# Moving the node tables and one-hots into place by DMA, and a second product tap for two channel groups

## The reference

```python
y = affine(conv1x1(x, fc1_w, fc1_b), fc1_s, fc1_t)
nodes = windows of y                                  # 64 nodes per window
idx = knn_idx(nodes, 9)                               # the 9 nearest nodes of each node
x_j = nodes[idx]; x_i = nodes[:, :, None, :]
feat = concat([x_i, x_j - x_i])
h = gelu((einsum('bnkc,oc->bnko', feat, ew) + eb) * es + et)
h = max(h, axis=2)                                    # over the 9 neighbours, 192 channels
x = affine(conv1x1(h, fc2_w, fc2_b), fc2_s, fc2_t) + x
```

```python
h = relu(bn(conv1x1(x, w1)))                          # 96 -> 576 channels
h = relu(bn(depthwise 3x3 (h, wd)))                   # 9 taps per channel
x = x + bn(conv1x1(h, w2))                            # 576 -> 96 channels
```

## Time and profile before

| | us |
|---|---|
| median of 3 runs | 4107.27 |
| lowest, highest | 4103.47, 4110.96 |
| the profiled execution, its own time | 4102.94 |
| its span, first to last instruction | 4101.1 |

### The profile page before, as it was taken

How to read it: one execution, slowest core, us unless ns; L and a number is a source line. 1 busy time by engine, 2 the same in 40 slices (tenths; PEclk the granted TensorE clock), 3 DMA queues, 4 the chain that set the end, 5 groups by cost and what they waited for, 6 DMA issues and landing times.

```text
span 4101.1 us, 79112 instructions
## 1 busy us (share of the span) xinstructions
PE 3901.0 (95%) x22752; PEld 2049.0 (50%) x22752; DVE 3821.5 (93%) x5162; ACT 3694.2 (90%) x6805; POOL 931.2 (23%) x1060
## 2 busy tenths in 40 slices
PE   4999999999999999999999999999999999999984
PEld 2445555455554555555555455555555455555542
DVE  2599999999999999999999999999999999999996
ACT  3899999999998999989999899989999899999983
POOL 0122222122222122222122222122222122222113
PEclk9999999999999999999999999999999999999996
DMA  1133342333333333343333333333333333433333
GB/s 50 24 64 76 58 88 51 67 76 66 73 73 66 60 75 73 58 80 57 69 75 66 73 61 75 62 69 76 62 79 57 70 66 67 81 61 59 62 66 65
DMA packets 100114, 272.31 MB, mean 66 GB/s; under 512 B 14946, under 2 KB 23394, under 8 KB 93476
## 3 DMA queue, kind: packets, MB, share of 16 engines
q0 software_dynamic: 65536, 184.58, 26.4%
q1 hardware_dynamic: 34116, 82.27, 7.5%
HBM read 77.68 MB, written 25.69 MB: 25 GB/s over the span
## 4 chain that ended last, share of the span: by engine, by line
PE 68%; DVE 11%; issue 9%; ACT 9%; DMA 1%; SPq 0%; POOL 0%; DVEq 0%; ACTq 0%; POOLq 0%
PE pg L648 18%; PE pmisc L576 9%; PE pg L651 8%; PE pvu L635 8%; DVE acc L1032 7%; PE pmisc L562 7%; PE pmisc L519 3%; PE pmisc L512 2%; PE pvu L621 2%; ACT MV L807 2%; PE pmisc L578 2%; DVE hid L1010 2%; PE pmisc L542 2%; PE pmisc L547 2%; ACT tapped L844 1%
## 5 line engine op out<-in xcount | busy, mean ns | idle before, releaser
L1032 DVE SCALAR_TENSOR_TENSOR acc<-hpad,w,acc 128x1024 f32<-128x1024 f32 (+1 forms) x2304 | 2618.2, 1160 | 33.5 <-issue 16.3
L648 PE MATMUL pg<-MV,VU 128*128 128x512 f32 x2048 | 1149.2, 643 | 40.7 <-ACT VU L815 29.8
L824 ACT ACTIVATE g<-pg 128x512 f32<-128x512 f32 x1536 | 912.5, 594 | 127.9 <-PE pg L651 81.4
L1010 DVE TENSOR_REDUCE hid<-g 128x192 f32<-128x1536 f32 x512 | 892.6, 1743 | 0.0
L429 POOL DMA_DIRECT2D acc<-tapped x256 | 241.3, 943 | 2106.8 <-DVE acc L1032 1818.8
L807 ACT ACTIVATE MV<-pvu,cst 64x512 f32<-64x512 f32 x1024 | 696.0, 680 | 11.8 <-PE pvu L621 5.0
L576 PE MATMUL pmisc<-acc,w 128*96 128x256 f32 x2048 | 497.1, 386 | 49.0 <-ACT acc L854 34.1
L651 PE MATMUL pg<-MV,VU 128*64 128x512 f32 x2048 | 527.5, 592 | 0.0
L562 PE MATMUL pmisc<-x,w 96*128 96x512 f32 (+1 forms) x1024 | 518.3, 608 | 7.0 <-ACT hpad L766 7.0
L635 PE MATMUL pvu<-wVU,y 97*64 97x192 f32 x4096 | 446.7, 339 | 21.8 <-ACT MV L807 21.2
L576 PEld LDWEIGHTS pmisc<-acc,w 128*96 128x96 f32 x2048 | 331.5, 165 | 262.6 <-issue 154.9
(11 more groups left out here) (101 smaller groups left out, 4447.6 us busy)
## 6 DMA issues: line engine op xcount, KB each, us to landing
acc<-tapped POOLq DMA_DIRECT2D x256, 512.0 KB, 4.9
xin<-in_x_dram SPq DMA_DIRECT2D x32, 768.0 KB, 5.8
invb<-rows_dram SPq DMA_DIRECT2D x32, 768.0 KB
x<-in_x_dram POOLq DMA_DIRECT2D x128, 192.0 KB, 4.4
res<-x POOLq DMA_DIRECT2D x128, 192.0 KB, 5.0
out_dram<-res SPq DMA_DIRECT2D x128, 192.0 KB, 3.2
hpad<-hpad SPq DMA_DIRECT2D x112, 33.0 KB, 1.8
g<-in_consts_dram SPq DMA_DIRECT2D x1, 640.0 KB
```

Of the source, the lines that this page charges most:

```text
L648: last = nc.tensor.matmul(ps[:, :], VU[:, r, part, 0:ONE128], cols[part], start=True, stop=True)
L824: nc.scalar.activation(g[:, p % 2, part, :, :], pg[(3 * p + part) % 2][:, :].rearrange("p (n k) -> p n k", k=KN), ACT.Gelu).then_inc(gelu_ ...
L1010: nc.vector.tensor_reduce(hid[:, c % 2, j, :, :], g[:, r], op=ALU.max, axis=AX.X).then_inc(hid_ready, 1)
L1032: nc.vector.scalar_tensor_tensor(out=dst, in0=src, scalar=wk, in1=dst, op0=ALU.mult, op1=ALU.add).then_inc(tap_done, 1)
```

## The change

**Part 1, the pair's path.** Both blocks of 64 partitions are computed where they fall, and SP's DMAs carry them to where `gather` wants them:

- `values` is one matmul of 384 columns into 128 partitions, one pair earlier (of P+2 in the slot of P); `vu_copy` copies it into the new tile `nodesVU`; four DMAs of 64 partitions by 192 values (`move_tables`) bring it into `VU`.
- `onehot` is one ScalarE instruction over 128 partitions into the new tile `onehots`; two DMAs of 64 partitions by 512 values, 128 KB each (`move_onehots`), bring it into `MV`.
- `gather` waits for these DMAs (`onehot_moved`, `vu_moved`) instead of ScalarE.
- On SP, the store and the broadcast of the norms stand in two slots instead of one, and result stores and the upper edge rows one slot later.

```diff
+            def move_tables(P, p):
+
+                if due(count := 3 * P - 3):
+                    sp.wait_ge(gather_ready, count)
...
+                if due(count := P + 1):
+                    sp.wait_ge(vu_evac, count)
...
+                for k in range(2):
+                    for w in range(2):
+                        sp.dma_start(VU[64 * k:64 * k + 64, p % 2, w, :], nodesVU[64 * w:64 * w + 64, k, :]).then_inc(vu_moved, 16)
+
+            def move_onehots(P, p):
+
+                if due(count := P + 1):
+                    sp.wait_ge(onehot_ready, count)
...
+                for w in range(2):
+                    sp.dma_start(MV[0:64, p % 2, w, :], onehots[64 * w:64 * w + 64, :]).then_inc(onehot_moved, 16)
...
+                    if valid(P + 1, NPAIRS):
+                        move_tables(P + 1, p + 1)
+                        move_onehots(P + 1, p + 1)
...
-                for w in range(2):
-                    nodes = y[:, c, o + NODES * w:o + NODES * (w + 1)]
-                    for k in range(2):
-
-                        h = 64 * (w ^ k)
-                        last = nc.tensor.matmul(pvu[h:h + 64, O * w:O * (w + 1)], nodes, wVU[:, k, :], start=True,
-                                                stop=True)
+                last = nc.tensor.matmul(pvu[:, 0:2 * O], y[:, c, o:o + 128], wVU[:, 0:2, :].rearrange("p k o -> p (k o)"),
+                                        start=True, stop=True)
...
-                        if due(count := P + 1):
-                            pe.wait_ge(onehot_ready, count)
-                        if due(count := P + 1):
-                            pe.wait_ge(vu_evac, count)
+                        if due(count := 32 * (P + 1)):
+                            pe.wait_ge(onehot_moved, count)
+                        if due(count := 64 * (P + 1)):
+                            pe.wait_ge(vu_moved, count)
...
-                for w in range(2):
-                    h = 64 * w
-                    last = nc.scalar.activation(MV[h:h + 64, p % 2, w, :].rearrange("p (n k) -> p n k", k=KN),
-                                                pone[h:h + 64, :, :].rearrange("p k n -> p n k"), ACT.Relu,
-                                                bias=nbias[h:h + 64, :], scale=1.0)
-                last.then_inc(onehot_ready, 1)
+                if due(count := 32 * P):
+                    act.wait_ge(onehot_moved, count)
+                nc.scalar.activation(onehots[:, :].rearrange("p (n k) -> p n k", k=KN), pone.rearrange("p k n -> p n k"),
+                                     ACT.Relu, bias=nbias, scale=1.0).then_inc(onehot_ready, 1)
```

```diff
-UPPER_AT, LOWER_AT = {2: FULL}, {5: FULL}
+UPPER_AT, LOWER_AT = {3: FULL}, {5: FULL}
...
-TAP_COUNTS = [3, 4, 4, 4, 5, 5, 5, 4, 2]
+TAP_COUNTS = [3, 3, 4, 4, 4, 5, 4, 4, 3]
+EARLY_PRODUCT_AT, EARLY_SUM_AT = {3: 2, 4: 3}, {4: 2, 5: 3}
...
-STORE_AT = {o + 2: q for o, q in W2_AT.items() if q % 2 == 1}
+STORE_AT = {o + 3: q for o, q in W2_AT.items() if q % 2 == 1}
...
+            def add_early(t, s, gr):
+
+                pool.wait_ge(early_done, 2 * s + gr - 1)
                 pool.sem_inc(pool_passed, 1)
                 nc.gpsimd.dma_start(acc[:, t % 2, sums_of(gr, 0, STRIP * W)], tapped[:, gr, :],
                                     accum_op=ALU.add).then_inc(tap_sum[gr], 16)
...
+            def early_product(b, p, s, gr):
+
+                if due(count := 16 * sums_before(s, gr)):
                     act.wait_ge(tap_sum[gr], count)
                 nc.scalar.activation(tapped[:, gr, :].rearrange("p (row col) -> p row col", col=W),
...
+                if k == 1 and gr in (2, 3):
+                    dve.wait_ge(tap_sum[gr], 32 * s + 16)
+                elif k == 1:
```

102 lines of the change are left out of this document (63 added, 39 removed).

## The result

| | median us | runs | lowest to highest | ratio to before | profiled span us, granted clock |
|---|---|---|---|---|---|
| before | 4105.37 | 4 | 4101.32 to 4110.96 | | 4101.1, 0.987 |
| after | 5222.66 | 4 | 5206.65 to 5243.15 | 1.272 (1.267 to 1.277) | 5205.0, 0.876 |

The change costs 1117 us. Slower was forecast, by 256 us; the time lies far above the range, whose upper end was 4480.

The account below looks back on a forecast made before the run. PE was taken as the bound, busy 981 of 1000 us. From 4101 us, gains of 73 and added one-hot waits of 329 (5.3 a strip) gave a span of 4357, 4363 as measured time; range 4230 to 4480, chance 0.60.

Parts of the forecast that it names:

- the bound: Whole kernel: PE bounds it, busy 981 of 1000 us in a steady stretch, with 1.9% left to gain from its waits.
- The formula: Slots 1 and 5: PE's wait is the one-hot DMA pair's duration less the room; 2.15 and 2.65 us a strip.
- the room of 2.74: Slot 1: time from the end of the one-hot instruction to the next pair's gather, 2.74 us; in slot 5, 2.25.
- For the pair: 0.47 + 3.9 = 4.4 us by L376's median: Slots 1 and 5: both one-hot DMAs under load, second issue plus an edge-row move's landing; raised to 4.9, range 3.8 to 6.4.
- almost the same: Profile after: PE's busy time in us would hardly change, its share falling to near 90%.
- have a whole slot and are hidden even under load: Tables' four DMAs, a pair ahead: issue 1.9 us, landing by 6 us of a 7.7 us slot, so no wait.
- (c): PE: one `values` matmul of 384 columns replaces four, 0.65 against 0.70 us, saving 0.4 us a strip.
- (d): PE's waits for the tables' copy and the one-hot instruction, 40.2 us over 60 strips, vanish: 0.67 us a strip.
- not the bound either: VectorE: two taps less save 2.3 of 59 us a strip, but it does not bound, except in the tail.
- The long way: Rival: the one-hot pair takes 6.4 us, waits 3.7 and 4.15, 8.3 us a strip, 4549 us; chance 0.04.
- In time: Rival: one-hots land within the room in slots 1 and 5, no wait; 4034 us, up to 4060; chance 0.17.

Follow-up runs that it names:

- all adds small: The changed kernel with all of POOL's accumulating DMAs cut to a sixteenth, the rest not added: 4243.09 us, ratio 1.035.
- half the columns: The changed kernel with each one-hot DMA moving only 256 of 512 columns of its 64 rows, the rest not moved: 5056.05 us, ratio 1.232.
- half the rows: The changed kernel with each one-hot DMA moving only 32 of its 64 rows, the rest not moved: 5051.43 us, ratio 1.231.
- Tables only: The kernel before with only the tables by one matmul and four DMAs a pair ahead; one-hots in place, taps as before: 4330.11 us, ratio 1.056.
- Tables two ahead: The kernel before with only the tables moved by DMA, with a whole pair more lead; one-hots in place, taps as before: 4062.78 us, ratio 0.989.
- two queues: The changed kernel with the second one-hot DMA of a pair issued by ScalarE on its own queue, the first by SP: 5208.81 us, ratio 1.268.
- small sums: The changed kernel with each of POOL's 512 KB sums cut to 64 of 1024 columns, the rest not added: 4606.92 us, ratio 1.123.
- half sums: The changed kernel with each of POOL's sums cut to 512 of 1024 columns, the rest not added: 4834.49 us, ratio 1.178.

## Why the prediction was wrong

**Right: the bound, the direction, the mechanism, the places.** The gather waits for the DMA into `MV`, in slots 1 and 5, next to nothing in 0, 3 and 7. One-hots take 351.0 us on ScalarE (said: about 350). The formula held in slot 1: 7.85 us from one-hots to gather, less the room of 2.74, gives 5.1 us of wait; measured 5.4. In slot 5, 7.2 less 2.25 gives 5.0, where 4.0 were measured, so the room there was about 3.2 us and not 2.25.

**Wrong: the duration put into it, 4.9 us, where 7.85 and 7.2 were measured.** The step that failed is "For the pair: 0.47 + 3.9 = 4.4 us by L376's median" and "so I go half a microsecond above the median, 4.9". Two errors are in it. The idle value was 3.2 and not 2.3 us (slot 5 of all adds small): a one-hot DMA lands after 2.2 us at the least, not after L381's 1.8. And of the two loaded rows I took the larger DMA because its size was nearer. Its bytes hardly matter, as half the columns shows, and its packets no more, as half the rows shows; what runs on the other queue does, and that the second DMA comes behind the first. In the trace of before, L376 is issued in slot 1 in 35 of 48 cases, with 192 KB adds in flight, and lands after a median of 3.8 us; L374 (4.4 to 6.2 us) is issued in slot 2, about 2 us behind a 512 KB sum. In the 11 cases in which L376 stands in slot 2 too, its median is 5.9 us as well. So the place decides, and the smaller DMA was the nearer row. And L376's maximum, 6.7, was in the same row and was not used as a bound. One one-hot DMA lands after a median of 6.2 us in slot 1 and 6.1 in slot 5 (said: 3.5 to 5) and of 2.3 in slot 3 (said: 1.8). With 7.5 us in place of 4.9 the sum has 10.0 us of waits in slots 1 and 5, where 9.4 were measured.

**Wrong: PE's busy time "almost the same".** This was never argued, only assumed, and it is 503 us, nearly half the loss. A row spoke against it: in the tail PE is half idle and the granted clock is 0.69, against 0.99 where it works without gaps. A wait of PE has a price beyond its length: 9.4 us of long waits a strip brought 8.2 us of longer work behind them. Without the 503 us the span would be about 4700 us, still above the range: both errors were needed for 5205, and the first alone was enough to leave it.

**Wrong: the tables "have a whole slot and are hidden even under load".** Tables only costs 225 us, with PE's waits for `VU` in slot 2. "Landing by 6 us of 7.7" left 1.7 us, and slot 2, behind the sums of slot 1, takes them. In after itself this is covered by the one-hots' waits (23.0 us at L695 for `VU`). One more pair of lead removes it.

**Mis-sized: the gains.** Tables two ahead measures terms (c) and (d) alone: 42 us where 55 were put for the waits of the earlier trace rows with the one matmul (0.4 and, of the 0.67, 0.5 us a strip). The matmul saved nothing: PE's busy time rose by 4.5 us, and from its start to the next matmul's it is 0.74 us in after's timeline (0.65 estimated; the four took 0.70). The gain is the vanished wait for the tables. The second product, 2.3 us less of VectorE a strip, costs 30 us alone and 52 beside tables two ahead; "not the bound either" was right, but ScalarE had no room for it.

**The rivals.** "The long way" was closest in kind, 4549, but its 6.4 us was too short and it had no clock in it; it had 0.04. "In time" had 0.17, on the thought that SP's packets pass between the sums'. They do, and it doesn't save them: the sum in progress lets none pass, the first DMA's four packets per engine wait for 0.34 us each and more, and the second DMA begins only as the next sum runs out. The Trainium skill ("DMA: Bandwidth & Descriptors", section "Queues, rings and completion order") has each DMA engine alternate between its queues by packets. The trace agrees for the second stretch (64 to 62) and not for the first, where all packets of the sum in progress went ahead; there the measurement decides. I had cited this rule in the prediction and not multiplied it out, and the rows that I called agreement, L376 against L381, show that a DMA is late and nothing of its packets. The same page's "Rules for kernel authors" says that two transfers to disjoint partition halves serialize, from one queue or from two. From one queue they did, one behind the other (2.6 to 4.8 us and from 5.0 on). From two they went side by side, and the second landed 1.0 us sooner in slot 5, but slot 1's wait grew by 0.7 us and the time was the same within 0.3%.

**What stays open.** Why a sum in progress lets none of SP's packets pass while the next one does, and why the second of two DMAs of one queue stays behind until that sum runs out. Why two queues made slot 1 later. And slot 1's wait of 3.2 us with small sums was put down to the 192 KB adds by cutting them all at once, not one at a time.

## What to carry over

Price a DMA that a saturated engine waits for by its slowest landing beside the largest transfer of the place where it will be issued, not by its median nor by its size. More lead can make it free: the tables' DMAs cost 225 us with one slot of lead and nothing with two (4063 us in all). Where there is no such lead, as for the one-hots, leave the data to be written in place. And price the slower clock behind a wait of TensorE: here mean waits of 3.2 to 6.1 us, over all these runs, made the next slot 2.8 to 5.1 us longer, and one of 2.0 us (half sums, slot 5) still 1.7, unless the engine was kept at work in the wait. And when a part is free alone, ask what it puts into the slot in which the other part is late.

## What the hardware showed that I had not expected

- After waits of 5.4 and 4.0 us (means), PE worked at the 1.2 GHz level for about 10 and 7 us (0.50 in the rows above), 1291 us in all against 108 before. Filling the waits with 9 unneeded matmuls a strip made the kernel 412 us faster.
- A DMA of SP of 128 KB lands in 2.2 us at the least and in up to 10.6 beside POOL's accumulating DMAs. In slot 5 it first waits for the one in progress, then goes packet for packet with the next, and the second of two waits until that one runs out. Halving its packets or its bytes gave the same (5051 and 5056 us); halving or quartering the sums gave far more (4834 and 4825).
- A wait on one queue spreads: ScalarE's tap 0 (L881) waited 223.8 us for SP's edge rows, issued behind the one-hots. What this cost by itself was not measured; PE's waits for ScalarE's Gelu at L695 are 21.7 us in all.
- One matmul of 384 columns to 128 rows took slightly longer from its start to the next than four of 192 columns to 64 rows each: 0.74 against 0.70 us.
